# Last cross attention: from phases per half of the batches to one pipeline over 32 units, with relative terms slanted through DRAM

## The reference, cut to what matters

```python
q = _heads(x @ Wq)
sim = jnp.einsum('bihd,bjhd->bhij', q, k) * SCALE
dist = jnp.clip(arange(77)[None, :] - arange(nq)[:, None], -16, 16) + 16
sim = sim + jnp.einsum('bihd,ijd->bhij', q, rel_k[dist]) * SCALE
attn = jax.nn.softmax(sim, axis=-1)
out = jnp.einsum('bhij,bjhd->bihd', attn, v) + jnp.einsum('bhij,ijd->bihd', attn, rel_v[dist])
out = out + stream(Wk_ip, Wv_ip, ctx_i) * (tanh(alpha) + 1) + stream(Wk_ap, Wv_ap, ctx_a) * (tanh(beta) + 1)
out = out.reshape(b, nq, INNER) @ Wo + bo
```

## Time and profile before

| | |
|---|---|
| median of three runs | 2743.32 us |
| span of the profiled execution | 2747.7 us |
| this sublayer, first projection to the next one's start | 2230.8 to 2667.3 us |
| TensorE, VectorE, ScalarE, GpSimd busy in the span | 88%, 52%, 41%, 27% |
| mean granted TensorE clock | 0.937 of full |

### The profile page before, as it was taken

How to read it: one execution, slowest core, us unless ns; L and a number is a source line. 1 busy time by engine, 2 the same in 40 slices (tenths; PEclk the granted TensorE clock), 3 DMA queues, 4 the chain that set the end, 5 groups by cost and what they waited for, 6 DMA issues and landing times. The chain is left out here.

```text
span 2747.7 us, 48070 instructions
## 1 busy us (share of the span) xinstructions
PE 2425.4 (88%) x18022; PEld 1804.3 (66%) x18024; DVE 1424.7 (52%) x3052; ACT 1135.2 (41%) x2771; POOL 737.6 (27%) x839
## 2 busy tenths in 40 slices
PE   7989869999797989769999799997899989899885
PEld 5767655665575977636666378886465658868772
DVE  5767402223564867612222456665665736515748
ACT  4468422222675635412222333333764643313415
POOL 4556241111353531040111111222101112201325
PEclk9999779999898999779999899998899999999998
DMA  5000442114101100331111500002000021202200
GB/s 177 2 2 2 188 180 62 45 46 174 63 2 49 47 1 2 143 134 74 46 45 37 217 1 1 1 1 93 1 1 1 1 85 55 70 0 70 62 3 31
DMA packets 61439, 152.34 MB, mean 55 GB/s; under 512 B 8974, under 2 KB 36750, under 8 KB 56145
## 3 DMA queue, kind: packets, MB, share of 16 engines
q1 hardware_dynamic: 52094, 122.23, 12.9%
q0 software_dynamic: 9120, 27.04, 2.7%
HBM read 101.46 MB, written 47.78 MB: 54 GB/s over the span
## 5 line engine op out<-in xcount | busy, mean ns | idle before, releaser
L3782 POOL TENSOR_TENSOR l3x_Pn<-l3x_Pn,l3x_fac 128x616 f32<-128x616 f32 (+2 forms) x96 | 70.3, 761 | 286.7 <-DVE l3x_fac L3832 286.7
L2108 POOL TENSOR_TENSOR l2a_Pn<-l2a_Pn,l2a_rden 128x1024 f32<-128x1024 f32 x32 | 60.1, 1897 | 295.5 <-DVE l2a_rden L2350 295.5
L1678 DVE TENSOR_TENSOR l1f_work<-l1f_work,l1f_psU 128x512 f32<-128x512 f32 x55 | 37.8, 687 | 191.8 <-PE l1f_psU L1426 167.0
L1442 PE MATMUL l1f_psY<-l1f_W,l1f_hT 128*128 (+1 forms) x440 | 106.1, 385 | 25.6 <-ACT l1f_hT L1539 25.6
L1533 ACT ACTIVATE l1f_work<-l1f_psG 128x512 f32<-128x512 f32 x55 | 32.8, 597 | 213.3 <-PE l1f_psG L1419 190.7
L1442 PEld LDWEIGHTS l1f_psY<-l1f_W,l1f_hT 128*128 128x128 f32 x440 | 81.4, 193 | 42.6 <-ACT l1f_hT L1539 26.5
L1351 POOL DMA_INDIRECT results_by_token<-l1f_rows_in_out,l1f_dest x39 | 37.4, 959 | 265.0 <-DVE l1f_rows_in_out L1689 265.0
L1351 POOL DMA_INDIRECT results_by_token<-l0f_rows_in_out,l0f_dest x39 | 37.2, 955 | 230.4 <-DVE l0f_rows_in_out L1689 230.4
L1678 DVE TENSOR_TENSOR l0f_work<-l0f_work,l0f_psU 128x512 f32<-128x512 f32 x39 | 26.8, 687 | 128.2 <-PE l0f_psU L1426 128.2
L885 ACT ACTIVATE l1a_att_Pn<-l1a_att_psS,l1a_att_nmx 128x128 f32<-128x128 f32 x256 | 91.8, 418 | 1.7 <-DVE l1a_att_nmx L1004 1.7
L885 ACT ACTIVATE l0x_Pn<-l0x_psS,l0x_nmx 128x128 f32<-128x128 f32 x256 | 91.7, 418 | 0.9 <-DVE l0x_nmx L1004 0.9
(11 more groups left out here) (784 smaller groups left out, 7128.2 us busy)
## 6 DMA issues: line engine op xcount, KB each, us to landing
l1f_W<-in_l1f_w SPq DMA_DIRECT2D x9, 1536.0 KB, 19.7
l0f_W<-in_l0f_w SPq DMA_DIRECT2D x8, 1536.0 KB
rows_by_expert<-zeros SPq DMA_DIRECT2D x2, 5011.5 KB, 26.7
l3x_K<-keys SPq DMA_DIRECT2D x16, 512.0 KB, 4.0
values<-l1f_W SPq DMA_DIRECT2D x11, 512.0 KB
l0f_rows_in_out<-rows_by_expert SPq DMA_DIRECT2D x39, 128.5 KB, 2.1
l1f_rows_in_out<-rows_by_expert SPq DMA_DIRECT2D x39, 128.5 KB, 2.1
l3x_V<-values SPq DMA_DIRECT2D x16, 308.0 KB
```

Of the source, the lines that this page charges most:

```text
L1442: ins = nc.tensor.matmul(psY[:, 0:D], hT[n % 2][:, j * P:(j + 1) * P], weights(n, 2 * DC * F + j * D, D), start=(j == 0), stop=(j == FC - 1))
L1678: nc.vector.tensor_tensor(h[n % 2], sg[n % 2], psU[:, :], ALU.mult).then_inc(h_ready, 1)
L2108: nc.gpsimd.tensor_tensor(part, part, rden[b % 2][:, 8 * u:8 * u + 8].unsqueeze(2).to_broadcast([P, 8, P]), ALU.mult)\
L3782: nc.gpsimd.tensor_tensor(v, v, fac[n % 3][:, s * HH:(s + 1) * HH].unsqueeze(2).to_broadcast([P, HH, SEG[s]]), ALU.mult)\
```

## The change

The phases per group are gone. One loop, `for it in range(-8, UN + 2)` with `UN` = 32, runs over all units on every engine; q is projected eight units ahead into a ring (`RING = 8` batches).

Relative keys: TensorE multiplies q of a unit (64 x 96 queries) by the table of differences `rkd` (64 x 32), once for each head. ScalarE puts the 32 values into a row of 172 per head: 80 zeros before, the last value repeated after (`extend`). SP stores the 96 rows to DRAM and loads them back with a row stride shorter by one, so that row i is shifted by i: that is the relative scores, 96 x 8 x 77. VectorE adds them into the scores' banks. Rows from 96 on are saturated, and a constant over a row leaves the softmax as it is.

Relative values: running sums of the weights along a row (a scan on VectorE in place of the three sums) are stored to DRAM and loaded back slanted, 96 x 8 x 32 (`near`). GpSimd masks and scales them, TensorE transposes them (`transpose_near`) and multiplies them by the table of steps rv[d] - rv[d+1] into the bank of the output; the constant rest of the table is one product (`end_rows`) added to the bias. The PSUM banks `psT` (two), `psO` and `psM` have no second set.

The core of the diff, in the order SP's functions and loop, TensorE's loop, ScalarE's loop, GpSimd's loop, VectorE:

```diff
+        def near_weights(n):
+            i = n % 2
+            sp.wait_ge(sums_ready, n + 1)
+            past(sp, near_loaded[i], 16 * (n // 2))
+            sp.dma_start(G.CD[i, EDGE:].rearrange("(r e) -> r e", e=HH * P), cum[i][0:ROWS, :]).then_inc(cum_stored[i], 16)
+            sp.wait_ge(cum_stored[i], 16 * (n // 2 + 1))
+            past(sp, near_masked, n - 1)
+            past(sp, near_ready, n - 1)
+            slanted = bass.AP(tensor=G.CD.tensor, offset=G.CD[i, EDGE - MAXREL:].offset, ap=[[HH * P + 1, ROWS], [P, HH], [1, BAND]])
+            sp.dma_start(near[i][0:ROWS, :].rearrange("p (h d) -> p h d", h=HH), slanted).then_inc(near_loaded[i], 16)
+
+        def relative_scores(n):
+            i = n % 2
+            sp.wait_ge(ext_ready, 2 * (n + 1))
+            if n >= 2:
+                sp.wait_ge(rel_loaded[(n - 2) % NR], 16 * ((n - 2) // NR + 1))
+            sp.dma_start(G.RD[i].rearrange("(r e) -> r e", e=HH * EXT), ext[i][0:ROWS, :]).then_inc(ext_stored[i], 16)
+            sp.wait_ge(ext_stored[i], 16 * (n // 2 + 1))
+            past(sp, biased, n - NR + 1)
+            slanted = bass.AP(tensor=G.RD.tensor, offset=G.RD[i, ROWS - 1:].offset, ap=[[HH * EXT - 1, ROWS], [EXT, HH], [1, S0]])
+            sp.dma_start(rel[n % NR][0:ROWS, :].rearrange("p (h j) -> p h j", h=HH), slanted).then_inc(rel_loaded[n % NR], 16)
...
+        for it in range(-4, UN):
+            if it % 2 == 0 and it + 4 < UN:
+                load_keys((it + 4) // 2)
+            if it % 2 and it >= -1 and it + 1 < UN:
+                load_values((it + 1) // 2)
...
+            if 0 <= it + 1 < UN:
+                near_weights(it + 1)
+            if it + 4 < UN:
+                relative_scores(it + 4)
+            if it == UN - 8:
+                sp.wait_ge(q_done, UN)
                 sp.dma_start(S.w[0], A["l3f_W1"]).then_inc(S.loaded[0], 16)
...
+        for it in range(-8, UN + 2):
+            if 0 <= it < UN:
+                transpose_p(it)
+            if 0 <= it + 2 < UN:
+                scores(it + 2)
+            if it % 2 and it >= 3:
+                project_out((it - 3) // 2, it)
+            if 0 <= it - 1 < UN:
+                transpose_near(it - 1)
+            if 0 <= it + 4 < UN:
+                relative_keys(it + 4, it)
+            if 0 <= it - 1 < UN:
+                weigh(it - 1)
+            if it + 8 < UN:
+                project(it + 8, it)
+            if it == -5:
+                end_rows()
...
+        for it in range(-8, UN + 1):
+            if 0 <= it < UN:
+                take_pT(it)
+            if 0 <= it - 1 < UN:
+                take_nearT(it - 1)
+            if 0 <= it + 4 < UN:
+                extend(it + 4)
+            if 0 <= it - 1 < UN:
+                take_o(it - 1)
+            if it + 8 < UN:
+                take_q(it + 8)
+            if 0 <= it + 2 < UN:
+                exps(it + 2)
...
+        for it in range(-1, UN):
+            if it >= 0:
+                near_values(it)
+            if it + 1 < UN:
+                weights(it + 1)
...
+        def maxima(n):
             dve.wait_ge(s_done, n + 1)
+            dve.wait_ge(rel_loaded[n % NR], 16 * (n // NR + 1))
+            v = seg(psS[0:ROWS, (n % 2) * 1024:(n % 2 + 1) * 1024], 0)
+            nc.vector.tensor_tensor(v, v, rel[n % NR][0:ROWS, :].rearrange("p (h k) -> p h k", h=HH), ALU.add).then_inc(biased, 1)
+            dve.wait_ge(biased, n + 1)
...
+        def factors(n):
...
+            nc.vector.tensor_tensor_scan(cum[i][:, :], segments_begin[:, :], Pn[n % NP][:, :], 0.0, ALU.mult, ALU.add).then_inc(sums_ready, 1)
+            dve.wait_ge(sums_ready, n + 1)
+            for s in range(3):
+                step.sig(nc.vector.reciprocal(den[i][:, s * HH:(s + 1) * HH], seg(cum[i][:, :], s)[:, :, SEG[s] - 1]))
...
+        for it in range(-2, UN + 2):
+            if 0 <= it + 1 < UN:
+                factors(it + 1)
+            if it + 2 < UN:
+                maxima(it + 2)
+                subtract(it + 2)
+            if it % 2 and it >= 3:
+                add((it - 3) // 2)
+            if it % 2 == 0 and it >= 4:
+                row_stats((it - 4) // 2)
```

More of the change, by code:

```diff
@@ L3604, in _ @@
             sp.wait_ge(v_loaded[i], 48 * (NB // 2))
+            sp.wait_ge(near_loaded[i], 16 * (UN // 2))
+        for i in range(NR):
+            sp.wait_ge(rel_loaded[i], 16 * len(range(i, UN, NR)))
     @block.tensor
     def _(pe):
[L3608 to L3616, removed]
[L3617 to L3622 removed]
@@ L3624, in relative_keys @@
[L3624 to L3643, removed]
@@ new lines, in end_rows, with relative_keys @@
+        def end_rows():
+            pe.wait_ge(small_loaded, NSMALL)
+            pe.wait_ge(out_loaded, 16)
+            for j in range(IC):
+                ins = nc.tensor.matmul(psO[:, 0:D], rve[:, :], wo[:, j * D:(j + 1) * D], start=(j == 0), stop=(j == IC - 1))
+            ins.then_inc(end_done, 1)
+        def relative_keys(n, it):
+            b, jj = unit(n)
+            if n == 0:
+                pe.wait_ge(tables_ready, 1)
+            pe.wait_ge(q_taken, 4 * (n // 4) + 4)
+            past(pe, ext_ready, 2 * n)
+            past(pe, pt_taken, it + 1)
+            for l in range(4):
+                for half in range(2):
+                    ins = nc.tensor.matmul(psT[0:ROWS, half * 512 + l * BAND:half * 512 + (l + 1) * BAND],
+                                           qTv[rows(half), b % RING, 4 * jj + l, 0:ROWS], rkd[rows(half), :], start=True, stop=True)
+            ins.then_inc(near_k_done, 1)
@@ new lines, in _ @@
+        nc.gpsimd.memset(steps[:, :], 0.0).then_inc(const_ready, 1)
+        step.sig(nc.gpsimd.memset(inside[:, :], 1.0))
+        pool.wait_ge(const_ready, 4)
+        for s in range(3):
+            nc.gpsimd.memset(seg(segments_begin[:, :], s)[:, :, 0:1], 0.0).then_inc(const_ready, 1)
+        step.wait()
+        step.do(nc.gpsimd.affine_select(out=inside[:, :], in_=inside[:, :], compare_op=ALU.is_ge, fill=0.0,
+                                        base=-MAXREL, pattern=[[1, BAND]], channel_multiplier=1))
@@ new lines, in row_stats @@
+        def row_stats(b):
+            xb = G.x[:, b * D:(b + 1) * D]
+            dve.wait_ge(x_ready, b + 1)
+            step.sig(nc.vector.bn_stats(out=st6[:, b * 6:(b + 1) * 6], in_=xb))
+            step.sig(nc.vector.tensor_reduce(G.xmax[:, b:b + 1], xb, AX.X, ALU.max))
+            step.do(nc.vector.tensor_reduce(G.xmin[:, b:b + 1], xb, AX.X, ALU.min))
+            step.sig(nc.vector.bn_aggr(out=G.mv[:, b * 2:b * 2 + 2], in_=st6[:, b * 6:(b + 1) * 6]))
+        for it in range(-2, UN + 2):
[8 more added lines that the diff above has]
+                row_stats((it - 4) // 2)
+            if it in (UN - 7, UN - 6):
+                i = it - (UN - 7)
+                dve.wait_ge(S.loaded[i], 16)
+                for half in range(2):
```

409 lines of the change are left out of this document (200 added, 209 removed).

## The result

The changed kernel takes **2697.59 us** (median of four runs, 2693.03 to 2707.29), the kernel before beside it 2746.53 (2743.11 to 2751.06). The ratio is 0.9826, 95% interval 0.9802 to 0.9851: 49 us faster. Forecast were 2680 us, 63 us faster.

What follows compares the result with a forecast made beforehand. SP's serial chain of two landings, 10.5 us an iteration over TensorE's 8.5, was to bound: 69 + 304.5 = 373.5 us against 436.5, so 2743.3 - 63 = 2680 us. Its own range was 2645 to 2718, the whole range 2615 to 2762.

Steps and rivals of the forecast that it cites:

- SP's chain of two landings in series: SP waits each iteration for running sums, then extended scores, to land: 10.5 us an iteration, above TensorE's 8.5.
- an empty queue: SP's stores with nothing queued ahead: running sums land after 2.5 us, extended scores after 2.6; 6.5 us with issues.
- the small pieces: Slanted loads in SP's queue: 768 pieces each, 48 per engine at 35 ns, so 1.7 us a load.
- K's 1.6 us: In SP's queue ahead of the running sums' store: K's 144 packets keep the sixteen engines busy 1.6 us.
- 8.5 us a unit: TensorE's summed work per unit of eight heads after the change; 32 units would take 273 us if it were the bound.
- rival 3: TensorE waits about 2 us of 10.5, its clock falls, nothing is gained: 2743 us; chance 0.09 together with the shared-bank case.
- ramp: Sublayer's start, from projections to the first running sums ready to be stored: 26 us.
- iterations, weight loads included: SP's 29 iterations doing both halves at 10.5 us, 304.5, plus 7 for the last sublayer's two weight loads.
- the end: Three iterations with only the near half at VectorE's 7.5 us, 23, then 13 after the last sums.
- The signs named ahead: Profile after: sublayer about 374 us, SP waiting for both stores, starts 10 to 11 apart, TensorE about 80%, DMA above 0.6.
- 1 (TensorE decides): The queue hides the transfers and TensorE's 8.5 us a unit sets the pace: 2622 us; chance 0.24.
- 2 (dear pieces): Small pieces of the two slanted loads cost 62 ns per packet, 13.1 us an iteration: 2756 us, a loss; chance 0.17.

Runs made afterwards that it cites:

- three different edits on SP's chain: Each against the changed kernel: both stores issued before the waits, 0.9645; K and V loaded from ScalarE's queue, 0.9691; extended scores stored from ScalarE's queue, 0.9693.
- whole rows: Changed kernel with each row of a slanted load read as one contiguous piece of the same bytes, slant left out: 2635.48 us, ratio 0.9765.
- without K and V: Changed kernel with the loads of K and V moved from SP's queue to the end of ScalarE's iteration, in ScalarE's queue: 2618.73 us, ratio 0.9691.
- three times the narrow products: Changed kernel with TensorE's eight narrow products with the key table done three times in each unit: 2655.23 us, ratio 0.9831.
- both stores first: Changed kernel with SP issuing the stores of running sums and extended scores before both waits and slanted loads: 2604.10 us, ratio 0.9645.
- TensorE's added work: Products with the key table done three times, against the kernel where SP issues both stores before waiting: 2636.62 us, ratio 0.9759.
- K and V moved as well: Changed kernel with SP issuing both stores before its waits and ScalarE issuing the loads of K and V: 2650.72 us, ratio 0.9663.

## Why the prediction was right

**The bound.** SP's chain of two landings in series was to take 10.5 us a unit. From 2267.82 to 2582.43 there are 29 iterations in 314.6 us, where 311.5 were forecast. The two around the weight loads take 13.35 and 14.31, the other 27 take 10.63 in the mean, among them the 9.96 and 12.12 of the timeline above. That it bounds is shown from both sides, by added work of TensorE that costs next to nothing, and by three different edits on SP's chain, which gain 48, 35 and 35 us by the ratio (46, 22 and 35 by the sublayer's length). And from 2289 to 2545 SP waited for anything but its landings only once, for 0.4 us.

**Its terms, however, were off in both directions.** With an empty queue I took 2.5 and 2.6 us for the two stores from a 512 KB store; the fastest of 32 landed in 3.0 and 3.4. That is 1.3 too little. For the small pieces I took 35 ns per packet and engine from the earlier trace rows, 3.4 us for the two loads of an iteration, 3.0 of them as queue. That was a misreading. I divided the whole of the 2.5 us by the packets, but the sixteen engines were busy for only 70.2% of it, as another line of that view says:

```profile
q1 hardware_dynamic: 1133, 0.50, 70.2%
```

By it a packet took 24.8 ns. And the pieces of the changed kernel were cheaper still. The page gives a price: q1's packets took 18.1% of 16 x 2705.6 us, where before they took 12.9% of 16 x 2747.7, 2164 engine-us more. The large pieces account for 27.7 MB more; at K's 26 engine-us for 0.52 MB that is 1380 of it (an estimate), and the remaining 780 over 49,152 pieces are 16 ns each. The trace's records of single packets agree: 14 ns for those of 128 bytes and 22 for those of 308, together 1.7 us an iteration on each engine. With whole rows the same bytes still take 1.4, which is why that edit shortened the spacing by only 0.3: it took away the pieces, not the bytes. K's 1.6 us is not contradicted (without K and V the running sums land 1.3 sooner) but isn't shown by itself, since the extended scores then land 1.0 later. So 1.3 too little for the landings met 1.3 too much for the pieces (3.0 against 1.7): the two waits, forecast at 5.1 and 3.9, were 4.9 and 3.7. The sum came out well because the errors cancelled, which is luck and no method. No row of before showed a store of 96 rows.

**Pieces below 512 bytes.** The trace after has 60,599 packets under 512 bytes. One of 128 bytes took 14 ns and one of 4096 took 198, 9 against 21 bytes per ns, and whole rows made the kernel 15 us faster. The Trainium skill, "DMA: Bandwidth & Descriptors", section "Specifications", says that pieces below 512 B miss line rate; the direction agrees, and in this kernel the loss is too small to decide.

**TensorE.** 8.5 us a unit were summed; the sublayer shows 306.1 us for 32 units, 9.6 each, with the product for the last row in it and at a mean clock of 0.90 of 2.4 GHz. At full clock the narrow products were 0.80 for 1.04 forecast, the steps 0.75 for 0.65 (differences of starts). In the pair at clock 1.00 TensorE is busy 20.25 of 21 us, in others at 0.66 and 0.84 about 15. So the fall of the clock that rival 3 speaks of is there in part: after the wait of 5.43 us shown above eight transposes take 1.97 us, in the unit before 1.09. In the time it isn't seen: in 393 us around the sublayer the kernel with three times the narrow products has TensorE busy for 340 us at a mean clock of 0.92, the changed kernel 308 us at 0.90, and the time is nearly the same.

**Where the 14.8 us lie** (388.3 measured, 373.5 forecast):
- ramp 31.0 for 26. Up to the first store of extended scores it was right (12.4 us: 2236.8 to 2249.18). From there to VectorE's first addition at 2257.64 8.5 us passed for 5.3: the store again 0.8 dearer, and the first slanted load shares the queue with the next unit's store, issued 0.4 later. Then SP, which was waiting for the third unit's store, sent the first running sums late;
- iterations, weight loads included: 3.1. The running sums' store behind the two loads took 9.2 us to land;
- the end, 42.7 for 36. I let three units run at VectorE's 7.5; their stores are 11.2 and 9.5 apart, at a clock of 0.84, while GpSimd is busy 27 of 42.7 us. The quantisation takes 13.4 of these (3.9 + 5.7 + 1.9 + 1.9), and I had costed it at nothing since GpSimd had time. Here it has not: its near weights and the weighing stand behind it in order. That this is what the end waits for is read from the order; no run moved the quantisation.

**The signs named ahead.** SP waits for its two stores in every iteration, TensorE is busy 79% of the sublayer, and its longest waits are ahead of the transposes: as said. The sublayer is 388 us long and not 374, the share of the DMA engines is 0.52 over the sublayer and not above 0.6, and the starts are 9.5 to 12.6 us apart and not 10 to 11.

**Rivals.** 1 (TensorE decides) is false for this kernel, and becomes nearly true one edit later: with both stores first the ratio is 0.9645, 2646 by the median before, where the rival said 2622. 2 (dear pieces) false. 3 and 4: no sign in the time, though 3's low clock is there in places.

## What to carry to other kernels

A bounce through DRAM makes whoever waits for it pay the landing: here at the least 3.0 us for 384 KB and 3.4 for 516 KB, and 4.9 and 3.7 in the median of a busy queue. Two bounces in one iteration belong side by side: issue both stores, and only then wait for the first. Look for what a queue waits for between its issues; here two landings were 7.9 of SP's 10.7 us. When you price a packet from a busy stretch, take the share of it in which the engines were busy. And when a sum of terms agrees with the total, check the terms one by one before you trust them for the next kernel.

## What the runs showed of the hardware

**VectorE's scan and GpSimd hold each other up.** GpSimd's product with the mask, 96 x 256, reads and writes only its own tiles. In the changed kernel its 32 instances look so (first line, min/median/max in ns), and the timeline of VectorE and GpSimd shows one of the long ones:

```profile
L3848 POOL TENSOR_TENSOR l3x_near<-l3x_near,l3x_inside x32: 718/722/2786, 2274.8 to 2608.5; 96x256 f32<-96x256 f32 x32
```

```profile
2338.91 2.29 DVE L3934 TENSOR_TENSOR_SCAN l3x_cum<-l3x_segments_begin,l3x_Pn 128x1024 f32<-128x1024 f32 x1 [5.72 <-ACT l3x_Pn L3794]
2338.94 2.79 POOL L3848 TENSOR_TENSOR l3x_near<-l3x_near,l3x_inside 96x256 f32<-96x256 f32 x1 [6.42 <-DMA l3x_near<-cumulative_rows]
...
2599.04 1.90 POOL L3889 TENSOR_SCALAR l3f_w_w1q<-ctxT 128x2048 bf16<-128x2048 f32 x1
...
2599.98 3.08 DVE L3934 TENSOR_TENSOR_SCAN l3x_cum<-l3x_segments_begin,l3x_Pn 128x1024 f32<-128x1024 f32 x1 [0.80 <-ACT l3x_Pn L3794]
...
2601.01 2.57 POOL L3848 TENSOR_TENSOR l3x_near<-l3x_near,l3x_inside 96x256 f32<-96x256 f32 x1
```

The product started 0.03 after the scan and ended 0.53 after it, where others took 0.72 in all: it did most of its work after the scan's end. The later lines show the other direction: the scan started while GpSimd worked until 2600.94, and took 0.8 us longer than 2.29. With both stores first they meet more often (median 1196), with TensorE's added work still more (2326), and without the scan never:

```profile
L3858 POOL TENSOR_TENSOR l3x_near<-l3x_near,l3x_inside x32: 718/1196/2573, 2223.4 to 2511.3; 96x256 f32<-96x256 f32 x32
```

```profile
L3858 POOL TENSOR_TENSOR l3x_near<-l3x_near,l3x_inside x32: 718/725/730, 2221.7 to 2502.0; 96x256 f32<-96x256 f32 x32
```

(First both stores first, then the same with reductions in place of the scan.) All 32 are at 718 to 730 there, with every transfer unchanged, so it is the scan and not the DMA traffic. The Trainium skill, "SBUF — State Buffer", section "Who interferes with whom", says that a VectorE instruction with two inputs in SBUF contends with a GpSimd instruction that reads SBUF. The scan has two inputs in SBUF and GpSimd's product reads SBUF, and these lines agree. VectorE's three sums, which have one input, don't hold this product up in any of its 32 instances. Priced for the kernel: removing the scan gave 14 us in all, its longer time on VectorE included; I have not separated the two.

**The chip itself.** The same kernel of before took 2698 to 2701 us on two chips and 2743 to 2747 beside the changed kernel, 1.7% apart, as much as the whole change. The difference lies ahead of this sublayer, which starts 2180 to 2187 us into the span in the batches of the faster chips and 2224 to 2237 in the others. Whether the changed kernel's ratio is the same on the faster chips was not measured; its two ratios (0.9826 and 0.9818) are both from the slower side. With both stores first the sublayer takes 343.9 us on a faster chip and, with K and V moved as well, 343.8 on a slower one.
